# Diff attention: the rows for the maxima taken from the rounded parts of q and k, on 32-row tiles of TensorE

## The chip, the cores and the metric

The kernel runs on one core of one Trainium2 chip. The metric is the device time of one execution in microseconds (us); less is better. A core has TensorE (matrix products, written to PSUM banks), VectorE, ScalarE, GpSimd and SyncE, each with an instruction queue of its own that it works off in order, and they meet at semaphores.

## What is computed

The reference is a two-layer decoder on x of 4 x 512 x 512 floats: windowed attention, context attention, a table-lookup feed-forward, diff attention, a state-space scan and a mix. The change lies in diff attention alone, which is this (batch 4, T = 512, E = 512, 16 heads; q1, k1, q2, k2 have 16 features per head, v has 32):

```python
qkv = layernorm(x) @ W_attn
lam = exp(dot(lambda_q1, lambda_k1)) - exp(dot(lambda_q2, lambda_k2)) + LAMBDA_INIT
attn1 = einsum('bthd,bshd->bhts', q1, k1) * scale
attn2 = einsum('bthd,bshd->bhts', q2, k2) * scale
score = softmax(attn1 - lam * attn2, axis=-1)
out = einsum('bhts,bshd->bthd', score, v)
return ((1 - LAMBDA_INIT) * out.reshape(B, T, E)) @ W_proj
```

With q1 scaled and q2 scaled by -lam, the difference of the two products is one product over 32 features per head: [q1, -lam q2] against [k1, k2]. The softmax subtracts a row maximum before the exponential; whatever number is subtracted cancels in the quotient, so it need only be near the maximum.

## The kernel before

The stages run one after another with a barrier between them. Diff attention (`stage_diff_attention`) is the fourth of five. It makes one pass for each of the 4 batch entries; in a pass the 16 heads go in 4 groups of 4 heads (HG = 4, E2 = 32 features each, so that 4 heads fill 128 partitions). Three groups are in work at once: while group g gets its scores and its output, the row maxima of group g + 1 are found and q and k of group g + 2 are projected (`project`, L1602). The last groups of a pass do that for the first groups of the next one; the last pass has nothing after it.

q and k of a group come out of `project` with 4 heads on 128 partitions in one PSUM bank each. ScalarE writes the rounded value to the tile hi (`high`, L1741), VectorE the rest to the tile lo (`low`, L1814), which also frees the bank. SyncE then copies, head by head, three blocks of 32 partitions into qs and ks (`stack`, L1579): hi, lo, hi for q against hi, hi, lo for k. So qs and ks hold each head on 96 partitions, and a product over the 96 has nearly full precision in one pass of TensorE. Partition 96 of qs takes the negated row maximum, against ones in ks.

For each group there are 16 row steps, one for each head and each tile of 128 queries (`rows`, L1620): one matmul 96 x 128 against 96 x 512 into one bank. VectorE takes the maximum over its 512 columns (`maxima`, L1829) and frees the bank. When all 16 are there, TensorE transposes the maxima (`negate`, L1630), VectorE negates them (`negated`, L1836), and GpSimd's DMA puts them on partition 96 of qs (L1910). Only then can the scores of that group be made, transposed, with the maximum already subtracted (`columns`, L1638); ScalarE takes the exponential from two score banks of their own, and `weigh` (L1648) multiplies by v and by ones, four heads side by side on 32 columns each.

All of rows, q, k, the transposed maxima, and once a pass the transposed features, the values and the output products share one ring of four PSUM banks (`Ring`, L67): the steps listed in `steps` (L1531) take banks 0, 1, 2, 3, 0, ... in this order, and a step waits on `ring.free` of its bank until the step four places before it has been read out. TensorE's order within a group is written out in `one_pass` (L1663): for st = 0 and 1 it is columns, rows, project (q for st = 0, k for st = 1), columns, weigh over v, columns, rows, weigh over ones; then, after st = 1, negate, and then four more weighs with columns between them. ROWS_AT says which row steps go in each of the four places: 0 and 1 ahead of q, 2 to 6 after it, 7 to 10 ahead of k, 11 to 15 after it. VectorE's order (L1852) is: finish of the group before (`finish`, L1844: the reciprocal of the sums and the product with them), maxima of the first place, low of q, maxima of the second and third place, low of k, maxima of the fourth, negated. In the first group of a pass it then does the layer norm of the next pass, in the second it copies features; the additions to x (L1876) stand at the end of a pass.

Of the kernel before, what the change touches and what calls it, by code (L numbers as in the profile page):

```python
# [24 lines left out]
ALU = mybir.AluOpType  # L25
# [7 lines left out]
P = 128  # L33
# [1454 lines left out]
def stage_diff_attention(core, sb, psum, dram, x, consts, scratch):  # L1488
# [21 lines left out]
    hi = sb("d_hi", [P, 2, T], F32R)  # L1510
# [15 lines left out]
    ROWS_AT = ((0, 2), (2, 7), (7, 11), (11, 16))  # L1526
# [39 lines left out]
    with nc.Block() as block:  # L1566
        @block.sync
        def _(sp):
# [10 lines left out]
            def stack(ring, in_pass, g):  # L1579

                for n, (rows, parts) in enumerate(((qs, (hi, lo, hi)), (ks, (hi, hi, lo)))):
                    b, turn = ring.at(("qk"[n], g), in_pass)
                    sp.wait_ge(ring.free[b], turn + 1)
                    for block_, part in enumerate(parts):
                        for j in range(HG):
                            sp.dma_start(rows[block_ * E2:(block_ + 1) * E2, g * HG + j, :].bitcast(F32),
                                         part[j * E2:(j + 1) * E2, n, :].bitcast(F32)) \
                                .then_inc(stacked[n], 16)
# [11 lines left out]
        def _(pe):  # L1600
# [19 lines left out]
            def rows(ring, in_pass, g, a, z):  # L1620

                for m in range(a, z):
                    j, tt = m // TT, m % TT
                    b, turn = ring.at(("row", g, m), in_pass)
                    pe.wait_ge(ring.free[b], turn)
                    nc.tensor.matmul(banks[b][:], qs[0:3 * E2, g * HG + j, tt * P:(tt + 1) * P],  # L1626
                                     ks[0:3 * E2, g * HG + j, :], start=True, stop=True) \
                        .then_inc(ring.full[b], 1)
# [34 lines left out]
            def one_pass(i, more):  # L1663
                for g in range(GROUPS):
# [3 lines left out]
                    if rows_on:  # L1668
                        for m in range(2):
# [48 lines left out]
            for tt in range(TT):  # L1718
                values(first, 0, tt)
            for m in range(2):  # L1720
# [8 lines left out]
        def _(act):  # L1729
# [11 lines left out]
            def high(ring, in_pass, n, kind, g):  # L1741
# [6 lines left out]
                nc.scalar.activation(hi[:, m, :], banks[b][:], ACT.Copy if m else ACT.Identity,  # L1748
# [52 lines left out]
        def _(dve):  # L1801
# [12 lines left out]
            def low(ring, in_pass, n, kind, g):  # L1814
# [5 lines left out]
                if m == 0:  # L1820
                    ins = nc.vector.scalar_tensor_tensor(
                        out=lo[:, m, :], in0=banks[b][:], scalar=coef[:], in1=hi[:, m, :].bitcast(F32),
                        op0=ALU.mult, op1=ALU.subtract)
                else:
                    ins = nc.vector.tensor_tensor(lo[:, m, :], banks[b][:], hi[:, m, :].bitcast(F32),
# [3 lines left out]
            def maxima(ring, in_pass, g, a, z):  # L1829
                for m in range(a, z):  # L1830
                    b, turn = ring.at(("row", g, m), in_pass)
                    dve.wait_ge(ring.full[b], turn)
                    nc.vector.tensor_reduce(mx[:, g, m // TT, m % TT:m % TT + 1], banks[b][:], AX_X, ALU.max) \  # L1833
# [372 lines left out]
```

## Time and profile before

| | |
|---|---|
| median of 3 runs | 2582.32 us (2578.64 to 2584.28) |
| the profiled execution | 2584.38 us |
| its span in the profile | 2582.6 us |
| TensorE matmuls busy | 88% of the span |
| VectorE busy | 69% |
| ScalarE, GpSimd busy | 36%, 41% |
| diff attention | from about 1870 to 2462 us |

The profile lists instructions by line of the kernel with their duration and the idle time of their engine before them. The timeline lists them in order of time, neighbours of one kind merged: "2134.61 3.60 PE L1608 ... x8" are eight matmuls of line 1608, the first of which starts at 2134.61 us and the last of which ends 3.60 us later. A product of plain floats takes two matmul records for each matmul of the code; one of the rounded type takes one. PE is TensorE, DVE is VectorE.

### The profile page before, as it was taken

To read this page: it belongs to the slowest core of one execution; us is meant where nothing else is said; L and a number is where in the kernel's file an instruction comes from. 1 tells how busy PE (TensorE), PEld (TensorE's weight loads), DVE (VectorE), ACT (ScalarE), POOL (GpSimd) and SP (SyncE) were. 2 spreads that over 40 slices of the span, in tenths; PEclk is the share of its full clock that TensorE was granted. 3 is DMA by queue.
4 is the path that set the end of the run, shared out by engine and by line. 5 is a ranking of instruction groups with operands and counts; after the bars stand their busy time and mean duration, and the time that the engine had idled before them with its cause. 6 is when DMAs were issued, how large, how long until landed. Compare 5 with 4: busy or idle time off the path is not lost. (4 is left out here: it accounts for less than half of the span.)

```text
span 2582.6 us, 24445 instructions
## 1 busy us (share of the span) xinstructions
PE 2262.6 (88%) x6992; PEld 1049.2 (41%) x6992; DVE 1771.1 (69%) x2979; ACT 920.4 (36%) x1759; POOL 1052.6 (41%) x789
## 2 busy tenths in 40 slices
PE   6998998999899777774798989989869999999858
PEld 3554444455455443332243434334333333434224
DVE  1887687688768877773688897987745455554454
ACT  1443323334333323331554636446203323232311
POOL 2453333355333424443598888988700000000033
PEclk9999999999999988886899999999979999999878
DMA  6000000000000022225321222221142222121021
GB/s 245 18 21 17 17 25 21 17 17 21 21 17 25 22 88 82 82 82 198 116 91 53 86 83 82 91 77 62 49 131 50 50 49 49 40 58 34 16 98 53
DMA packets 88746, 158.34 MB, mean 61 GB/s; under 512 B 14912, under 2 KB 42432, under 8 KB 86352
## 3 DMA queue, kind: packets, MB, share of 16 engines
q1 hardware_dynamic: 72256, 139.76, 17.1%
q10 hardware_dynamic: 15888, 17.43, 2.1%
q8 instruction: 34, 0.56, 0.1%
q14 instruction: 56, 0.46, 0.1%
q0 software_dynamic: 512, 0.13, 0.0%
HBM read 101.18 MB, written 30.80 MB: 51 GB/s over the span
## 5 line engine op out<-in xcount | busy, mean ns | idle before, releaser
L1389 PE MATMUL c_bank<-c_xn_t,c_weights 128*128 128x512 f32 (+1 forms) x704 | 326.4, 609 | 21.1 <-ACT c_h_t L1429 19.5
L706 POOL TENSOR_SCALAR a_prob<-a_prob,a_rsum 128x256 f32<-128x256 f32 x256 | 147.1, 594 | 466.8 <-DVE a_rsum L634 466.6
L1287 DVE TENSOR_TENSOR_SCAN s_state<-s_decay,s_state 128x512 f32<-128x512 f32 x256 | 305.0, 1210 | 36.1 <-ACT s_decay L1221 36.1
L1237 POOL TENSOR_TENSOR s_state<-s_b_rows,s_delta_u 128x1024 f32<-128x1024 f32 x128 | 301.2, 2363 | 11.2 <-DMA s_b_rows<-scan_bc 8.8
L1221 ACT ACTIVATE s_decay<-s_delta,s_a 128x512 f32<-128x512 f32 x256 | 173.2, 688 | 296.5 <-DVE s_state L1287 269.4
L438 PE MATMUL a_bank<-a_xn_t,a_wq 128*128 128x512 f32 x512 | 227.2, 592 | 0.0
L521 PE MATMUL a_bank<-a_wo,a_out_t 128*128 128x512 f32 x512 | 222.3, 592 | 0.0
L1910 POOL DMA_DIRECT2D d_qs<-d_neg_t x16 | 8.2, 514 | 515.3 <-DVE d_neg_t L1841 515.3
L549 ACT ACTIVATE a_prob<-a_score,a_neg_m 128x256 f32<-128x256 f32 x256 | 117.8, 476 | 278.8 <-DVE a_neg_m L629 278.6
L320 DVE TENSOR_SCALAR f_picks<-f_mask,f_lut_xor,f_lut 128x260 int32<-128x260 int32 x512 | 202.5, 468 | 9.6 <-DVE f_mask L314 1.1
L1762 ACT ACTIVATE d_prob_t<-d_score 128x512 f32<-128x512 f32 x256 | 139.0, 595 | 194.5 <-PE d_score L1645 193.2
L1389 PEld LDWEIGHTS c_bank<-c_xn_t,c_weights 128*128 128x128 f32 (+1 forms) x704 | 128.7, 190 | 179.6 <-issue 176.8
L330 DVE COPY_PREDICATED f_picks<-f_mask,f_picks 128x260 int32<-128x260 int32 x448 | 177.7, 455 | 25.6
L1833 DVE TENSOR_REDUCE d_mx<-d_bank 128x1 f32<-128x512 f32 x256 | 158.6, 683 | 33.4 <-PE d_bank L1626 31.9
L1399 PE MATMUL c_bank<-c_weights,c_h_t 128*128 128x512 f32 (+1 forms) x352 | 168.7, 624 | 0.0
L1250 POOL TENSOR_TENSOR s_group<-s_group,s_state 128x1024 f32<-128x1024 f32 x64 | 151.8, 2372 | 12.5 <-DVE s_state L1295 12.2
L1295 DVE TENSOR_TENSOR s_state<-s_state,s_c 128x1024 f32<-128x1024 f32 x128 | 152.8, 1194 | 0.0
L521 PEld LDWEIGHTS a_bank<-a_wo,a_out_t 128*128 128x128 f32 x512 | 97.3, 190 | 122.5 <-issue 122.5
L438 PEld LDWEIGHTS a_bank<-a_xn_t,a_wq 128*128 128x128 f32 x512 | 97.3, 190 | 109.6 <-issue 108.1
L458 PE MATMUL a_score<-a_k_t,a_q_t 128*128 128x256 f32 (+1 forms) x512 | 132.2, 362 | 0.0
L1608 PE MATMUL d_bank<-d_xn_t,d_w 128*128 128x512 f32 x256 | 120.1, 615 | 4.0 <-ACT d_xn_t L1734 2.7
L1250 POOL TENSOR_TENSOR s_group<-s_state 128x1024 f32<-128x1024 f32 x32 | 75.2, 2350 | 111.0 <-DVE s_state L1295 110.9
(194 smaller groups left out, 3726.6 us busy)
## 6 DMA issues: line engine op xcount, KB each, us to landing
s_b_rows<-scan_bc SPq DMA_DIRECT2D x64, 512.0 KB, 3.6
f_idx<-in_idx SPq DMA_DIRECT2D x64, 130.0 KB, 2.1
ffn_weights<-f_picks SPq DMA_DIRECT2D x64, 130.0 KB, 1.8
r_factor<-in_factors SPq DMA_DIRECT2D x8, 1024.0 KB, 9.0
d_qs<-d_hi SPq DMA_DIRECT2D x128, 64.0 KB, 2.0
d_ks<-d_hi SPq DMA_DIRECT2D x128, 64.0 KB, 2.0
a_wo<-in_wo_t ACTq DMA_DIRECT2D x1, 4096.0 KB, 15.7
scan_y<-m_d_u SPq DMA_DIRECT2D x4, 1024.0 KB, 3.9
```

What stands on the lines that cost most here:

```text
L320: last = dve.tensor_scalar(picks[:, j, :], mask[:, 0, :], self.lut_xor[:, j:j + 1], self.lut[:, 2 * j:2 * j + 1], ALU.bitwise_and, ALU.bit ...
L330: last = self.nc.vector.copy_predicated(self.picks[:, j, :], self.mask[:, level + 1, :], self.picks[:, j + half, :])
L438: mm = nc.tensor.matmul(banks[b][:], w[:, k, :], xn_t[:, k, :], start=(k == 0), stop=(k == KD - 1))
L521: mm = nc.tensor.matmul(banks[b][:], out_t[:, tt, r * P:(r + 1) * P], wo[:, g * REPS + r, :], start=(r == 0), stop=(r == REPS - 1))
L1221: self.nc.scalar.activation(self.decay[u % 2][:], self.delta[:, h % 2, e, :], ACT.Exp, scale=self.a[:, h % 2 * 2 + e, n:n + 1]).then_inc(s ...
L1237: pool.tensor_tensor(self.state[:, s], row.broadcast_to([P, 2, T]), self.delta_u[:, h % 2], ALU.mult) \
L1250: pool.tensor_tensor(group, old if n == 1 else group, self.state[:, c % self.SLOTS], ALU.add) \
L1287: dve.tensor_tensor_scan(self.state[:, s, e, :], self.decay[u % 2][:], self.state[:, s, e, :], 0.0, ALU.mult, ALU.add).then_inc(self.scann ...
L1295: dve.tensor_tensor(self.state[:, s], self.state[:, s], row.broadcast_to([P, 2, T]), ALU.mult) \
L1389: mm = nc.tensor.matmul(banks[b][0:width[o], :], weights[:, lo:lo + width[o]], xn_t[:, k, :], start=(k == 0), stop=(k == KD - 1))
L1399: mm = nc.tensor.matmul(banks[b][:], h_t[0:width[o], o, tt * P:(tt + 1) * P], weights[0:width[o], W_DOWN + o * D:W_DOWN + (o + 1) * D], st ...
L1833: nc.vector.tensor_reduce(mx[:, g, m // TT, m % TT:m % TT + 1], banks[b][:], AX_X, ALU.max) \
```

## The change

The tile hi is kept twice, for even and odd groups, so that hi of group g + 1 still stands while hi of group g + 2 is written. `stack` copies from the copy of its group, `high` and `low` write and read it. The row steps no longer read qs and ks on 96 partitions; they read hi itself, head j on partitions 32 j to 32 j + 31, as matmuls of 32 rows. Their order is turned: m now runs over the four heads of one query tile first (tt, j = divmod(m, 4)), so that four neighbouring steps lie on four different row tiles of the array, and each writes a bank of its own. The maxima are thus those of the product of the rounded parts. ROWS_AT becomes four places of four steps: 0 to 3 ahead of q, 4 to 7 after it, 8 to 11 ahead of k, 12 to 15 after it. Since the rows now read what ScalarE wrote, TensorE waits for hi_done; the wait for the copies (stacked) stays where it is. The number of matmuls, maxima and copies is the same.

```diff
@@ -1507,7 +1507,7 @@
     coef = sb("d_coef", [P, 1], F32)
     norm = Norm(core, sb, "d")
     xn_t = sb("d_xn_t", [P, KD, T], F32)
-    hi = sb("d_hi", [P, 2, T], F32R)
+    hi = sb("d_hi", [P, 2, 2, T], F32R)
     lo = sb("d_lo", [P, 2, T], F32R)
     qs = sb("d_qs", [P, DH, T], F32R)
     ks = sb("d_ks", [P, DH, T], F32R)
@@ -1523,7 +1523,7 @@
     acc = psum("d_acc", [P, T], F32)
     acc_sum = psum("d_acc_sum", [P, T], F32)
     ROWS = HG * TT
-    ROWS_AT = ((0, 2), (2, 7), (7, 11), (11, 16))
+    ROWS_AT = ((0, 4), (4, 8), (8, 12), (12, 16))
     xn_steps = [("xn", k) for k in range(KD)]
     v_steps = [("v", tt) for tt in range(TT)]
     rows_steps = lambda g, a, z: [("row", g, m) for m in range(a, z)]
@@ -1578,7 +1578,8 @@
 
             def stack(ring, in_pass, g):
 
-                for n, (rows, parts) in enumerate(((qs, (hi, lo, hi)), (ks, (hi, hi, lo)))):
+                high = hi[:, g % 2]
+                for n, (rows, parts) in enumerate(((qs, (high, lo, high)), (ks, (high, high, lo)))):
                     b, turn = ring.at(("qk"[n], g), in_pass)
                     sp.wait_ge(ring.free[b], turn + 1)
                     for block_, part in enumerate(parts):
@@ -1620,12 +1621,12 @@
             def rows(ring, in_pass, g, a, z):
 
                 for m in range(a, z):
-                    j, tt = m // TT, m % TT
+                    tt, j = divmod(m, HG)
+                    head = slice(j * E2, (j + 1) * E2)
                     b, turn = ring.at(("row", g, m), in_pass)
                     pe.wait_ge(ring.free[b], turn)
-                    nc.tensor.matmul(banks[b][:], qs[0:3 * E2, g * HG + j, tt * P:(tt + 1) * P],
-                                     ks[0:3 * E2, g * HG + j, :], start=True, stop=True) \
-                        .then_inc(ring.full[b], 1)
+                    nc.tensor.matmul(banks[b][:], hi[head, g % 2, 0, tt * P:(tt + 1) * P], hi[head, g % 2, 1, :],
+                                     start=True, stop=True).then_inc(ring.full[b], 1)
 
             def negate(ring, in_pass, g):
 
@@ -1666,6 +1667,7 @@
                     rg, pg = (g + 1) % GROUPS, (g + 2) % GROUPS
                     rows_on, proj_on = more or g + 1 < GROUPS, more or g + 2 < GROUPS
                     if rows_on:
+                        pe.wait_ge(hi_done, (n + 2) * 2)
                         for m in range(2):
                             pe.wait_ge(stacked[m], (n + 2) * COPIES + 1)
                     for st in range(TT):
@@ -1717,6 +1719,7 @@
                 pe.wait_ge(w_in[n], 16)
             for tt in range(TT):
                 values(first, 0, tt)
+            pe.wait_ge(hi_done, 2)
             for m in range(2):
                 pe.wait_ge(stacked[m], COPIES + 1)
             rows(first, 0, 0, 0, ROWS)
@@ -1745,7 +1748,7 @@
                 act.wait_ge(stacked[m], n * COPIES + 1)
                 b, turn = ring.at((kind, g), in_pass)
                 act.wait_ge(ring.full[b], turn)
-                nc.scalar.activation(hi[:, m, :], banks[b][:], ACT.Copy if m else ACT.Identity,
+                nc.scalar.activation(hi[:, g % 2, m, :], banks[b][:], ACT.Copy if m else ACT.Identity,
                                      scale=1.0 if m else coef[:]).then_inc(hi_done, 1)
 
             def exponentials(n, st, half):
@@ -1819,10 +1822,10 @@
                 b, turn = ring.at((kind, g), in_pass)
                 if m == 0:
                     ins = nc.vector.scalar_tensor_tensor(
-                        out=lo[:, m, :], in0=banks[b][:], scalar=coef[:], in1=hi[:, m, :].bitcast(F32),
+                        out=lo[:, m, :], in0=banks[b][:], scalar=coef[:], in1=hi[:, g % 2, m, :].bitcast(F32),
                         op0=ALU.mult, op1=ALU.subtract)
                 else:
-                    ins = nc.vector.tensor_tensor(lo[:, m, :], banks[b][:], hi[:, m, :].bitcast(F32),
+                    ins = nc.vector.tensor_tensor(lo[:, m, :], banks[b][:], hi[:, g % 2, m, :].bitcast(F32),
                                                   ALU.subtract)
                 ins.then_inc(ring.free[b], 1)
 
@@ -1830,7 +1833,8 @@
                 for m in range(a, z):
                     b, turn = ring.at(("row", g, m), in_pass)
                     dve.wait_ge(ring.full[b], turn)
-                    nc.vector.tensor_reduce(mx[:, g, m // TT, m % TT:m % TT + 1], banks[b][:], AX_X, ALU.max) \
+                    tt, j = divmod(m, HG)
+                    nc.vector.tensor_reduce(mx[:, g, j, tt:tt + 1], banks[b][:], AX_X, ALU.max) \
                         .then_inc(ring.free[b], 1)
 
             def negated(ring, in_pass, n, g):
```

## Rows read from the trace of the kernel before

**Rows 1.** The page: TensorE busy, and the granted clock in 40 slices.

```profile
PE 2262.6 (88%) x6992; PEld 1049.2 (41%) x6992; DVE 1771.1 (69%) x2979; ACT 920.4 (36%) x1759; POOL 1052.6 (41%) x789
...
PEclk9999999999999988886899999999979999999878
```

**Rows 2.** Groups by line, 1870 to 2475 us: busy us, mean ns, idle before, releaser.

```profile
L1833 DVE TENSOR_REDUCE d_mx<-d_bank 128x1 f32<-128x512 f32 x256 | 158.6, 683 | 33.4 <-PE d_bank L1626 31.9
...
L1626 PE MATMUL d_bank<-d_ks,d_qs 96*128 96x512 f32 x256 | 82.3, 421 | 3.5
...
L1635 PE MATMUL d_bank<-ident,d_mx 128*16 128x128 f32 x16 | 4.4, 277 | 16.3 <-DVE d_mx L1833 16.3
```

**Rows 3.** Windows of 30 us: width, busy of PE, PEld, DVE, ACT, POOL, PEclk, DMA.

```profile
2150.00:2180.00 30.00, 27.46 (x127) 10.73 (x125) 18.54 (x26) 10.79 (x20) 0.49 (x1) 1.00 0.26 62
```

**Rows 4.** Timeline of TensorE, third group of the second pass: start, length, what.

```profile
2134.61 3.60 PE L1608 MATMUL d_bank<-d_xn_t,d_w 128*128 128x512 f32 x8
...
2140.31 1.68 PE L1626 MATMUL d_bank<-d_ks,d_qs 96*128 96x512 f32 x5
2141.92 1.06 PE L1659 MATMUL d_acc_sum<-d_prob_t,ones 128*32 128x512 f32 x8
2142.91 0.74 PE L1645 MATMUL d_score<-d_qs,d_ks 97*128 97x512 f32 x2
2143.49 1.09 PE L1626 MATMUL d_bank<-d_ks,d_qs 96*128 96x512 f32 x4
2144.68 3.70 PE L1608 MATMUL d_bank<-d_xn_t,d_w 128*128 128x512 f32 x8
...
2149.87 1.68 PE L1626 MATMUL d_bank<-d_ks,d_qs 96*128 96x512 f32 x5
...
2153.53 0.27 PE L1635 MATMUL d_bank<-ident,d_mx 128*16 128x128 f32 x1 [0.99 <-DVE d_mx L1833]
```

**Rows 5.** Timeline of VectorE in the same group.

```profile
2136.34 1.28 DVE L1833 TENSOR_REDUCE d_mx<-d_bank 128x1 f32<-128x512 f32 x2
...
2140.74 5.67 DVE L1833 TENSOR_REDUCE d_mx<-d_bank 128x1 f32<-128x512 f32 x9 [0.91 <-PE d_bank L1626]
...
2150.30 3.08 DVE L1833 TENSOR_REDUCE d_mx<-d_bank 128x1 f32<-128x512 f32 x5 [0.57 <-PE d_bank L1626]
```

**Rows 6.** Timeline, VectorE: fourth group of that pass, its finish and first maxima.

```profile
2159.04 3.36 DVE L1847 RECIPROCAL d_rsum<-d_acc_sum 128x512 f32<-128x512 f32 x1 [4.83 <-PE d_acc_sum L1659]
...
2163.05 1.28 DVE L1833 TENSOR_REDUCE d_mx<-d_bank 128x1 f32<-128x512 f32 x2
```

**Rows 7.** Timeline, TensorE: the rows and q of the fourth group.

```profile
2160.93 0.63 PE L1626 MATMUL d_bank<-d_ks,d_qs 96*128 96x512 f32 x2
2161.40 3.60 PE L1608 MATMUL d_bank<-d_xn_t,d_w 128*128 128x512 f32 x8
```

**Rows 8.** Timeline: second group of that pass, q on TensorE, first maxima on VectorE.

```profile
2106.00 3.60 PE L1608 MATMUL d_bank<-d_xn_t,d_w 128*128 128x512 f32 x8
...
2108.92 1.28 DVE L1833 TENSOR_REDUCE d_mx<-d_bank 128x1 f32<-128x512 f32 x2
```

**Rows 9.** Timeline: first group of that pass, first maxima and q.

```profile
2079.20 1.28 DVE L1833 TENSOR_REDUCE d_mx<-d_bank 128x1 f32<-128x512 f32 x2
2079.22 3.60 PE L1608 MATMUL d_bank<-d_xn_t,d_w 128*128 128x512 f32 x8
```

**Rows 10.** Timeline, VectorE: third group of the last pass, which projects nothing.

```profile
2409.05 8.85 DVE L1833 TENSOR_REDUCE d_mx<-d_bank 128x1 f32<-128x512 f32 x14 [2.25 <-PE d_bank L1626]
```

**Rows 11.** Timeline, TensorE, scan stage: a 32-row matmul between full ones.

```profile
1301.14 0.50 PE L1174 MATMUL s_c<-s_c_parts,s_c_pick 32*128 32x512 f32 x1
1301.57 1.12 PE L1389 MATMUL c_bank<-c_xn_t,c_weights 128*128 128x512 f32 x2
```

**Rows 12.** Windows, TensorE alone: width, busy, PEclk, DMA share, GB/s.

```profile
2402.00:2405.50 3.50, 2.27 (x7) 1.00 0.02 5
2406.00:2409.00 3.00, 3.00 (x12) 0.50 0.00 0
2426.50:2433.00 6.50, 5.88 (x20) 0.50 0.01 3
360.40:366.00 5.60, 2.83 (x19) 1.00 0.16 48
```

**Rows 13.** Timeline, SyncE: the last copies of k, third group.

```profile
2154.74 2.49 SPq L1586 DMA_DIRECT2D d_ks<-d_lo  x4
```

## What the change will do to the time

> **What bounds the kernel now.** Only diff attention is touched. The page says that TensorE is the busiest engine, near full clock from the middle of this stage on [rows 1]. The stretches of the stage narrow it: in 30 us TensorE has 27.5 us of matmuls, VectorE 18.5, ScalarE 10.8 [rows 3]. So TensorE sets the pace, and VectorE, at under two thirds, looks as if it had room. The grouping by line says where TensorE stops: the row matmuls take 82.3 us of records, with 3.5 us of idle time before them, and the transposed maxima (line 1635) have 16.3 us before them, all of it for VectorE's maxima [rows 2]. The timeline of one group then shows how the two engines are tied: TensorE's steps [rows 4] stand beside VectorE's maxima [rows 5]. What has to be read off is which maximum frees the bank of which matmul, since that is what the change moves.
>
> **What TensorE saves.** Row matmuls of 96 rows follow each other by (1.09 - 0.39)/3 = 0.23 us [rows 4], where 0.39 us is the length of one. Sixteen are 3.7 us a group. Four side by side should take the time of one: four sets, 0.9 us. Against that stand the changes of tiling. The only 32-row matmul in the trace occupies TensorE from 1301.14 to 1301.57, 0.43 us instead of 0.23 [rows 11]: 0.2 us to go in and out. The weigh, four tiles of 32 columns beside each other, takes 0.99 us to the next instruction for two times 0.43 us of stream: 0.13 us [rows 4] (0.43 us from q's eight records: 3.60 us less one record of 0.59, over seven). Two of the four sets stand ahead of a projection (two more changes each), two ahead of a weigh (one more), so I take 0.1 us for going in and up to 0.8 us a group in all. Pure TensorE time: -2.8 + 0.8 = -2.0 us a group, some -29 us for the 15 groups whose rows lie inside the passes. This holds only where TensorE doesn't wait, so every place has to be gone through.
>
> **Place 1, ahead of q.** Before, rows 0 and 1 take two banks and q takes a third. After, rows 0 to 3 take all four, and q takes the bank of row 0: it can't start before VectorE has reduced row 0. But VectorE is then in the finish of the group before, which waits for that group's last weigh and stands ahead of the maxima. In the fourth group of the second pass the reciprocal starts at 2159.04, takes 3.36 us, and the first maximum starts at 2163.05 [rows 6], while q started at 2161.40 [rows 7]. One maximum takes 0.68 us [rows 2], and 0.15 us pass from a maximum to the matmul that waits for it (next paragraph). So q starts at 2163.05 + 0.68 + 0.15 = 2163.88, later by 2.48 us. In the third group: 2136.34 + 0.83 = 2137.17 against 2134.61 [rows 4, 5], 2.56 us. In the second group a layer norm stands ahead of the finish too: 2108.92 + 0.83 = 2109.75 against 2106.00, 3.75 us [rows 8]. In the first group no finish, only the last addition to x: 2079.20 + 0.83 against 2079.22, 0.81 us [rows 9]. TensorE has nothing else to do in that time: behind q in its queue stand columns and weigh, ScalarE waits for those, and hi and lo of q come later too.
>
> **Place 2 and k.** Before, k takes the bank of row 7, the sixth of the nine maxima that start at 2140.74 and follow by (5.67 - 0.68)/8 = 0.62 us: 2140.74 + 5 x 0.62 + 0.68 = 2144.52, and k starts at 2144.68 [rows 4, 5]; that is the 0.15 us. After, k takes the bank of row 8, the fifth maximum behind the start of place 2. In the third group place 2 starts 2.56 + 0.1 us later, so the maxima start at 2143.40, and k at 2143.40 + 4 x 0.62 + 0.68 + 0.15 = 2146.71, which is 2.03 us late: 0.53 us are won back. What the sets save on TensorE is worth nothing here, VectorE's maxima are what ends last. Row 7 needs q's bank; its lo is done before place 2 starts, as before.
>
> **Place 4 and negate.** Before, five maxima from 2150.30, after it four, from 2150.30 + 2.03 + 0.1 = 2152.43. The last ends at 2152.43 + 3 x 0.60 + 0.68 = 2154.91, negate starts at 2155.06 against 2153.53 [rows 4, 5]: 1.53 us late, 0.50 us won back. From there the group runs as before, and the next one starts with this delay.
>
> **Sum of the waits.** Second groups 3.75 - 1.03 = 2.72, third 1.53, fourth 2.48 - 1.03 = 1.45, in three passes: 17.1 us. The last pass has one more group with finish and q and without the norm, 1.45. First groups 0.81 - 1.03 = -0.22, four of them, -0.9. The third group of the last pass projects nothing; there fourteen maxima run without a break up to negate [rows 10], and twelve will: -2 x 0.63 + 0.1 = -1.15. Together +16.5 us. The first sixteen rows of the stage are bound by VectorE before and after, 0. The wait on hi_done costs nothing, the wait on the copies beside it comes later. The second copy of hi adds no instruction. The copies of k end by about 2157.2 + 2 [rows 13] and the next group's wait for them is passed at about 2160; low of k moves by 0.5 us more than negate, still hidden.
>
> **The clock.** The new waits are long. The granted clock has fallen in this stage after short work with gaps: from 2402.00 to 2405.50 TensorE is busy 2.27 us of 3.50, waiting for ScalarE and then for the finish; after it, from 2406.00 to 2409.00, the clock is at 0.50, 1.2 instead of 2.4 GHz [rows 12]. Another stretch at 0.50 lasts from 2426.5 to 2433.0. On the other side 2.8 us of idle time between long dense matmuls left the clock at 1.00 [rows 12]. The new wait resembles the first case: ahead of it stand only two columns, a wait for ScalarE and the set of rows, then 2.5 us or more of nothing. I take it that the clock falls in most of the ten waits of 2.4 us and more. The price by the rows: at half clock for about 3.4 us, 1.7 us of matmuls are lost; for 6.8 us, 3.4. With 1.7 us each, 17 us; bounds 0 and 34.
>
> **The sum.** 16.5 + 17 = 33.5 us. On the profiled execution, 2584.4 us (span 2582.6), that gives 2618; on the median of the runs, 2582.3, 2616.
>
> The Trainium skill has two pages on this. "TensorE: Matmul & The Clock Gate", Part 3, gives 3.07 times the speed for four 32-row tiles of 512 columns; no row tiles stand side by side in this trace, and by it alone the rows' TensorE time would shrink to a third. "TensorEngine Tiling (Array Packing)", under PSUM Bottleneck, says that tiling makes TensorE faster but not the reading of PSUM; the maxima that end last before k and negate agree with it. Its Key Properties say that a change of tiling mode drains TensorE; the 0.2 us around the 32-row matmul agree.
>
> **Rivals.** (1) TensorE alone decides, and the bank of row 0 is free when q wants it: -2.0 us a group, 2582.3 - 29 = 2553 us. For it speaks that TensorE is busy 92% and VectorE 62% [rows 3]. It decides if VectorE's first maximum ends before the set of rows does, about 2161.5 in the fourth group; the finish ends 1.6 us after that point, so this needs another order of VectorE or of the ring than the text of the kernel has. (2) The waits are as above, but the clock doesn't fall: 2582.3 + 16.5 = 2599 us. The last of rows 12 speaks for it. (3) The four tiles don't run beside each other: 4 x 0.23 a set. The weigh behind places 2 and 4 then comes 0.7 us later, inside TensorE's waits for banks and for the last maximum; at most 0.2 us a group get through, 3 us, 2619 us. (4) The clock was hurt elsewhere before and this is better now, and gains and waits cancel: about 2582.
>
> **How the numbers follow.** Forecast with the clock's fall 0.66, rival 2 0.18, rival 1 0.07, rival 3 0.04, rival 4 0.05. The likeliest case runs from 2604 (clock falls in every other wait) to 2633 (the longer price each time). The range takes in rival 2 with 3 us for the settings that I have rounded, and leaves out the top: 2595 to 2628. Faster or slower by over 0.2% is about what a measurement of this kernel can tell from no change. Faster 0.07, within 0.2% 0.05, slower 0.88.
>
> **What would show it.** Right: ahead of q (the weight load or matmul of line 1608) idle time of 2.4 to 3.6 us in ten groups, put down to VectorE's maxima, none over 0.8 in first groups; four row matmuls starting within 0.3 us of each other; idle time ahead of line 1635 up from 16.3 us to some 28 us; stretches at 0.50 of the clock starting at the head of second, third and fourth groups; a distance of about 28 to 30 us between the heads of groups that was 26.8 us. Wrong: q starting right behind the rows, a group under 26.8 us, or the clock at 1.00 throughout. If the sets start 0.1 us apart or more, the tiles load one after another.

## The result and the profile after

The changed kernel takes 2619.57 us, median of 4 runs (2619.26 to 2620.22), against 2582.06 us for the kernel before (4 runs, 2578.64 to 2584.28): the ratio is 1.0147, 95% interval 1.0129 to 1.0164. It is slower by 37.5 us. The forecast was 2616 us in a range of 2595 to 2628. The profiled execution has a span of 2617.5 us against 2582.6.

The page of the changed kernel, its lines for busy time and granted clock, as in [rows 1]:

```profile
PE 2264.1 (86%) x6992; PEld 1027.8 (39%) x6992; DVE 1768.4 (68%) x2979; ACT 919.9 (35%) x1759; POOL 1051.6 (40%) x789
...
PEclk9999999999999988885999999999788999989979
```

All busy times are within about 2% of those before. The work is the same; what grew is the time in which TensorE waits or runs slowly. The page hardly shows the clock's part: in the last third of the span five slices are under 9 where [rows 1] has four.

Groups by line of the changed kernel, 1870 to 2505 us, as in [rows 2] (its lines 1609, 1628, 1636, 1646, 1660 and 1837 are 1608, 1626, 1635, 1645, 1659 and 1833 of the kernel before):

```profile
L1837 DVE TENSOR_REDUCE d_mx<-d_bank 128x1 f32<-128x512 f32 x256 | 157.0, 680 | 35.4 <-PE d_bank L1628 35.1
L1609 PE MATMUL d_bank<-d_xn_t,d_w 128*128 128x512 f32 x256 | 144.4, 718 | 29.9 <-DVE d_mx L1837 25.7 <-ACT d_xn_t L1737 2.7
L1628 PE MATMUL d_bank<-d_hi 32*128 32x512 f32 x256 | 53.3, 505 | 2.6 <-ACT d_v L1742 0.2
L1636 PE MATMUL d_bank<-ident,d_mx 128*16 128x128 f32 x16 | 4.4, 277 | 25.6 <-DVE d_mx L1837 25.6
```

Three things are to be seen. The row matmuls take 29 us less of records than the 82.3 before. The projections now have 29.9 us of idle time ahead of them, 25.7 of it for VectorE's maxima, and their mean record is 718 ns, which is a mixture of matmuls at full and at half clock. The transposed maxima wait 25.6 us instead of 16.3. So what TensorE saves on the rows comes back as waiting.

Timeline of TensorE in the changed kernel, third group of the second pass, to be read against [rows 4]:

```profile
2152.94 0.99 PE L1646 MATMUL d_score<-d_qs,d_ks 97*128 97x512 f32 x2 [0.71 <-ACT d_prob_t L1765]
2153.86 0.51 PE L1628 MATMUL d_bank<-d_hi 32*128 32x512 f32 x4
2156.70 5.28 PE L1609 MATMUL d_bank<-d_xn_t,d_w 128*128 128x512 f32 x8 [2.33 <-DVE d_mx L1837]
...
2164.16 0.51 PE L1628 MATMUL d_bank<-d_hi 32*128 32x512 f32 x4
2164.59 1.06 PE L1660 MATMUL d_acc_sum<-d_prob_t,ones 128*32 128x512 f32 x8
...
2166.26 1.47 PE L1628 MATMUL d_bank<-d_hi 32*128 32x512 f32 x4
2167.82 3.70 PE L1609 MATMUL d_bank<-d_xn_t,d_w 128*128 128x512 f32 x8
...
2173.11 0.51 PE L1628 MATMUL d_bank<-d_hi 32*128 32x512 f32 x4
2176.28 0.27 PE L1636 MATMUL d_bank<-ident,d_mx 128*16 128x128 f32 x1 [1.66 <-DVE d_mx L1837]
```

And VectorE at the head of that group, against [rows 5]:

```profile
2151.97 3.35 DVE L1851 RECIPROCAL d_rsum<-d_acc_sum 128x512 f32<-128x512 f32 x1
2155.35 0.69 DVE L1853 SCALAR_TENSOR_TENSOR d_out_t<-d_acc,d_rsum 128x512 f32<-128x512 f32 x1
2155.96 2.47 DVE L1837 TENSOR_REDUCE d_mx<-d_bank 128x1 f32<-128x512 f32 x4
...
2164.69 4.87 DVE L1837 TENSOR_REDUCE d_mx<-d_bank 128x1 f32<-128x512 f32 x8 [1.09 <-PE d_bank L1628]
```

The four row matmuls are in their banks at 2153.86 + 0.51 = 2154.37. VectorE is in the reciprocal until 2155.32 and in the product until 2156.04, only then does it reduce row 0 and free its bank, and q starts at 2156.70. The first projection takes 5.28 us in place of 3.60, because the clock has fallen. TensorE's windows of the changed kernel there (width, busy, PEclk, DMA share, GB/s):

```profile
2150.00:2156.00 6.00, 3.66 (x24) 1.00 0.00 0
2156.50:2159.50 3.00, 2.80 (x4) 0.50 0.00 0
2160.50:2164.00 3.50, 3.50 (x16) 1.00 0.00 0
```

The clock is at 2.4 GHz while TensorE is busy 61% of the first window, and at 1.2 in the second, right behind the wait.

### The profile page after: what moved, and what is told of

The parts are those of the page before. It is cut to its first block and busy times, and to the rows that moved or that the text cites. A ratio compares the mean times of both kernels' runs of the same rounds, so it can differ in the third digit from the quotient of the medians.

```text
span 2617.5 us, 24461 instructions
## 1 busy us (share of the span) xinstructions
PE 2264.1 (86%) x6992; PEld 1027.8 (39%) x6992; DVE 1768.4 (68%) x2979; ACT 919.9 (35%) x1759; POOL 1051.6 (40%) x789
## 5 line engine op out<-in xcount | busy, mean ns | idle before, releaser
L330 DVE COPY_PREDICATED f_picks<-f_mask,f_picks 128x260 int32<-128x260 int32 x448 | 177.6, 455 | 25.6
L1837 DVE TENSOR_REDUCE d_mx<-d_bank 128x1 f32<-128x512 f32 x256 | 157.0, 680 | 35.4 <-PE d_bank L1628 35.1
L1609 PE MATMUL d_bank<-d_xn_t,d_w 128*128 128x512 f32 x256 | 144.4, 718 | 29.9 <-DVE d_mx L1837 25.7
```

Of the source, the lines that this page charges most:

```text
L330: last = self.nc.vector.copy_predicated(self.picks[:, j, :], self.mask[:, level + 1, :], self.picks[:, j + half, :])
L1837: nc.vector.tensor_reduce(mx[:, g, j, tt:tt + 1], banks[b][:], AX_X, ALU.max) \
```

## The experiments

Each differs in one thing from the kernel before, the changed kernel or another experiment. They are told in the order of the questions. Each ratio is to the kernel before, run beside it; its median lay between 2576.76 and 2583.36 us on these occasions.

**Places or tiles?** The change has two parts: rows read hi on 32-row tiles, and four places of four steps. Each was put alone on the chip. First the places, with the old 96-row matmuls:

```diff
-    ROWS_AT = ((0, 2), (2, 7), (7, 11), (11, 16))     # kernel before
+    ROWS_AT = ((0, 4), (4, 8), (8, 12), (12, 16))
```

> The kernel before (96-row row matmuls on qs and ks, hi kept once) with one edit: the four places take rows 0-3, 4-7, 8-11, 12-15 as in the changed kernel. Theory (place: q waits for the bank of row 0, which stands behind VectorE's finish, and the clock falls in that wait): the 32-row tiles have nothing to do with the loss, so nearly all of it is here too. Waits as in the prediction without 0.1 us a set for the change of tiling, 13 to 16 us, and the clock's fall 10 to 23 us (the wait is shorter by up to 0.5 us, since four rows take 0.9 us of TensorE instead of 0.45): 2605 to 2620 us. Rival (the 32-row tiles or the second copy of hi cost the time): within 5 us of before, 2582.

Measured: 2613.74 us (2611.47 to 2615.70), ratio 1.0128 (1.0107 to 1.0150). Its third group, TensorE's timeline:

```profile
2150.50 1.08 PE L1626 MATMUL d_bank<-d_ks,d_qs 96*128 96x512 f32 x4
...
2153.43 5.40 PE L1608 MATMUL d_bank<-d_xn_t,d_w 128*128 128x512 f32 x8 [1.84 <-DVE d_mx L1833]
```

The result is as expected. There are no 32-row tiles and no second hi here, and yet q waits for the maximum and runs at half clock. The places alone make 33 of the 37.5 us. Then the tiles, with the old places:

```diff
-    ROWS_AT = ((0, 4), (4, 8), (8, 12), (12, 16))     # kernel after
+    ROWS_AT = ((0, 2), (2, 7), (7, 11), (11, 16))
```

> The changed kernel (32-row tiles, hi kept twice, heads side by side) with one edit: the four places are those of before again, rows 0-1, 2-6, 7-10, 11-15. Theory: q has a bank of its own again, no wait for the finish, no fall of the clock; the maxima on VectorE end last before k and negate as before, and TensorE's saving is lost in these waits: 2580 to 2587 us. Rival (TensorE alone decides, so its 2 us a group should show as soon as q does not wait): 2553 to 2560 us. Rival (the tiles cost): 2610 or more.

Measured: 2611.51 us (2609.34 to 2615.18), ratio 1.0120 (1.0098 to 1.0141). This was a surprise: the tiles alone cost about 31 us as well, with q back where it was. The two costs don't add, 33 and 31 make 37.5. Groups by line of this kernel, 1870 to 2500 us:

```profile
L1628 PE MATMUL d_bank<-d_hi 32*128 32x512 f32 x256 | 59.1, 529 | 23.6 <-DVE d_mx L1837 23.2 <-ACT d_v L1742 0.2
...
L1636 PE MATMUL d_bank<-ident,d_mx 128*16 128x128 f32 x16 | 4.8, 297 | 15.3 <-DVE d_mx L1837 15.3
```

The rows themselves now wait 23.2 us for the maxima (the fifth row of a place needs the bank of its first). TensorE's windows around the transposed maxima of the third group, which start at 2163.03, columns as before:

```profile
2160.50:2163.20 2.70, 1.65 (x11) 1.00 0.43 100
2163.60:2166.80 3.20, 3.20 (x12) 0.50 0.43 106
2167.20:2170.00 2.80, 2.80 (x25) 1.00 0.10 23
```

The clock falls here too, at another place: behind negate. In the kernel before, the same passage stayed at 1.00. Seven of the twelve stretches at half clock in this kernel start within about 0.5 us of negate. From 1920 us to the end of the stage TensorE is at half clock for 27.3 us before, 85.3 in this kernel and 81.9 in the changed one.

**Is about half of the loss the clock?** Matmuls were put into the wait ahead of q. They write a score bank whose content is overwritten afterwards, so they do nothing but keep TensorE at work.

```diff
+                        if st == 0 and g and proj_on:
+                            pe.wait_ge(exp_done[0], n * FILLS + 3)
+                            for k in range(5):
+                                nc.tensor.matmul(score[0][:], w[:, k % KD, 0:P], xn_t[:, k % KD, :],
+                                                 start=True, stop=True)
```

> The changed kernel with one addition: ahead of q, in the groups that wait for the finish (second, third, fourth), TensorE does five more matmuls of plain floats, 128 x 512, into a score bank that is free then and is overwritten right after: 5 x 0.43 = 2.1 us of work inside a wait of 2.3 us. Theory: the wait for the bank stays, but the engine is at work in it and the clock stays at 2.4 GHz; what is won is what the clock cost, 17 to 23 us: 2597 to 2603 us. If the clock has no part in the loss: 2620 us, or more where the added matmuls overrun the wait.

Measured: 2621.91 us (2620.54 to 2625.97), ratio 1.0167 (1.0144 to 1.0189). TensorE's timeline, second group of the second pass, and VectorE's at the same place:

```profile
2119.29 4.56 PE L1683 MATMUL d_score<-d_xn_t,d_w 128*128 128x512 f32 x10
2123.69 3.60 PE L1609 MATMUL d_bank<-d_xn_t,d_w 128*128 128x512 f32 x8
```

```profile
2120.89 2.47 DVE L1842 TENSOR_REDUCE d_mx<-d_bank 128x1 f32<-128x512 f32 x4
```

The expectation failed. Five plain-float matmuls are ten records, longer than the wait: q's bank is free at 2120.89 + 0.68 + 0.15 = 2121.72, and q starts at 2123.69, 2.0 us after. Every q behind a filler takes 3.60 us again, but the filler costs what the clock gives back. So it says little on the total. The next kernel has a filler that fits, `range(4 if g == 1 and more else 2)` in place of `range(5)`.

> The changed kernel with matmuls that fit inside q's wait: one matmul of plain floats counts as two records of 0.43 us, so the five of the run before took 4.3 us, not 2.1, and overran the wait by about 1.9 us in each of ten groups. Now four ahead of q in the second group of the first three passes (3.4 us in a wait of 3.5) and two in the other seven groups (1.7 us in 2.3). Theory: q starts where it does in the changed kernel but runs at 2.4 GHz, 22 us are won on its ten projections: 2598 to 2606 us. If the clock has no part in the loss: 2618 to 2622.

Measured: 2607.82 us (2602.75 to 2611.91), ratio 1.0096 (1.0079 to 1.0113), which is 11.8 us less than the changed kernel, and 2 us above the expected range. Third group, TensorE, and the projections over the stage:

```profile
2145.23 0.50 PE L1628 MATMUL d_bank<-d_hi 32*128 32x512 f32 x4
2145.66 1.98 PE L1683 MATMUL d_score<-d_xn_t,d_w 128*128 128x512 f32 x4
2148.07 3.70 PE L1609 MATMUL d_bank<-d_xn_t,d_w 128*128 128x512 f32 x8 [0.42 <-DVE d_mx L1842]
```

```profile
L1609 PE MATMUL d_bank<-d_xn_t,d_w 128*128 128x512 f32 x256 | 122.4, 625 | 8.1 <-DVE d_mx L1842 3.9 <-ACT d_xn_t L1742 2.7
```

q of this group starts 12.26 us after the transposed maxima ahead of it (2135.81 to 2148.07), exactly as in the changed kernel (2144.44 to 2156.70). The projections' records sum to 22.0 us less than in the changed kernel (144.4), with work added rather than removed: the clock, and not the projections, had made them long. Only 11.8 us reach the total. The clock now falls behind negate in six groups (at 1963.1, 2051.9, 2106.5, 2195.3, 2249.9 and 2311.3 us); in the changed kernel it does so in three of them (1965.4, 2207.7 and 2262.3), so three are new. From 1920 us to the end of the stage TensorE is at half clock for 58.0 us against 81.9, and half of that difference is 12.0 us, close to what the total shows. The kernel with the tiles alone has its falls at the same place; so this is most likely the tiles' own cost, coming up where the other is gone.

**What of the tiles' cost is clock?** The same filler, one matmul, ahead of negate, in the kernel with the tiles alone:

```diff
                         if st == 1 and rows_on:
+                            pe.wait_ge(exp_done[0], n * FILLS + 7)
+                            nc.tensor.matmul(score[0][:], w[:, 0, 0:P], xn_t[:, 0, :], start=True, stop=True)
                             negate(ring, i, rg)
```

> The run with the tiles alone (places of before, 2611 us) with one matmul of plain floats, 0.86 us, into a free score bank ahead of negate, where TensorE waits 1.0 us for the last maximum. Theory: most of that run's loss is the clock, which falls about negate because the sets of rows leave TensorE with less to do there; filled, it stays up: 2594 to 2602 us, and what remains over before is the 0.65 us a group for the sets. If the clock is not it, or falls elsewhere: 2608 us or more.

Measured: 2597.86 us (2591.52 to 2601.55), ratio 1.0053 (1.0036 to 1.0069), 13.7 us less than without it, inside the expected range. Four groups, from the transposed maxima of the third group of a pass to those of the next pass, take 137.9 us in both full turns, where the kernel with the tiles alone took 139.8 and 143.8 us and the kernel before 135.4 both times. So 2.5 us a turn, some 0.65 us a group, are not clock. By the distances in the last section they are the changes into and out of the 32-row mode, less what the sets save of TensorE's time. In the last pass the clock still falls.

**Do the tiles cost because they are fast, or because they are 32 rows?** My first reading was that TensorE saves time on the rows, which becomes idle time, and the idle time brings the clock down. If so, 32-row matmuls that are not side by side should cost nothing. Two kernels tried that. One has the tiles but goes head by head, so that neighbours are on the same tile:

```diff
-                    tt, j = divmod(m, HG)          # kernel with tiles, old places; rows and maxima
+                    j, tt = divmod(m, TT)
```

> The run with the tiles alone (32-row tiles, places of before, 2611 us) with one edit: the row steps go head by head again, so that neighbours lie on the same 32-row tile and do not run side by side. It keeps the changes of tiling mode and takes away the time that TensorE saves. Theory (the saved time turns into waits in which the clock falls): the clock stays up, and only the entries into the mode cost, 0.3 to 0.65 us in 15 groups: 2586 to 2592 us, faster than with the rows side by side. If the changes of mode alone cost what the tiles cost: 2605 us or more.

Measured: 2621.82 us (2619.12 to 2622.97), ratio 1.0143 (1.0126 to 1.0160); the expectation failed, and its other branch, 2605 or more, came true. A place still holds rows of two heads, so there remained some overlap, and this kernel did not decide it. The other is the kernel before with one bound changed, from 96 partitions to 32. Its rows read only the rounded parts of the first block (the first 32 of the 96 partitions), so the maxima are those of the changed kernel; all rows are on one and the same tile, none beside another:

```diff
-                    nc.tensor.matmul(banks[b][:], qs[0:3 * E2, g * HG + j, tt * P:(tt + 1) * P],
-                                     ks[0:3 * E2, g * HG + j, :], start=True, stop=True) \
+                    nc.tensor.matmul(banks[b][:], qs[0:E2, g * HG + j, tt * P:(tt + 1) * P],
+                                     ks[0:E2, g * HG + j, :], start=True, stop=True) \
```

> The kernel before with one edit: each row matmul reads only the first 32 of its 96 partitions in qs and ks, that is the rounded parts (partitions 0 to 31 for every head). All of them lie on the same 32-row tile, so none runs beside another and TensorE spends the same 0.22 us on each as before; only the rows used and the tiling mode differ. Theory A (the clock falls because TensorE's time ahead of negate gets shorter): it stays up here, and only the entries into the mode cost, 0.3 to 0.65 us in 15 groups: 2586 to 2594 us. Theory B (a matmul of 32 rows does less for the clock than one of 96 rows that takes the same time; the head-by-head run, 2622 us, points to it): the clock falls about negate here too, 2602 to 2622 us.

Measured: 2616.34 us (2614.75 to 2620.37), ratio 1.0166 (1.0135 to 1.0196). TensorE's timeline, third group of the second pass:

```profile
2165.11 1.77 PE L1626 MATMUL d_bank<-d_ks,d_qs 32*128 32x512 f32 x5
2166.81 1.06 PE L1659 MATMUL d_acc_sum<-d_prob_t,ones 128*32 128x512 f32 x8
...
2168.87 0.37 PE L1635 MATMUL d_bank<-ident,d_mx 128*16 128x128 f32 x1 [0.99 <-DVE d_mx L1833]
```

This is inside the range of Theory B. The wait ahead of line 1635 is 0.99 us, as in [rows 4]. The places themselves are longer: five row matmuls take 1.70 us to the next instruction, against 1.61 in [rows 4], and in place 2 the columns ahead of them 0.80 instead of 0.71. Between transposed maxima (line 1635) without a fall of the clock lie 27.62 and 29.64 us where the kernel before has 26.69 and 28.71: 0.93 us a group for four places, 0.23 us a place, is the price of going into the 32-row mode and out of it. In 15 groups that is some 14 us of the 40 that this kernel loses to the kernel before. The rest is the clock. TensorE's windows at this place, first of the kernel before and then of this one; the first row of each pair is the 3.40 us up to the transposed maxima:

```profile
2150.13:2153.53 3.40, 2.31 (x13) 1.00 0.35 82
2153.50:2160.00 6.50, 6.08 (x39) 1.00 0.34 80
```

```profile
2165.47:2168.87 3.40, 2.32 (x13) 0.93 0.40 94
2168.50:2175.00 6.50, 6.13 (x25) 0.50 0.35 82
```

TensorE's records fill the same time ahead of the transposed maxima (2.32 us of 3.40 against 2.31; over 6.60 us 5.52 against 5.51), and its clock falls all the same, at 2168.4, 0.5 us ahead of them: 25 matmuls in the next window where there were 39. Over the stage it is 88.7 us at half clock against 27.3. So it is shown that 32-row matmuls cost the clock here though none runs beside another, though TensorE saves no time by them, and though there is neither a second hi nor a wait on hi_done: my first reading was wrong, and the second copy of hi is not needed for the loss. Side by side, in the kernel with the tiles alone, they cost less (31 us) than on one tile. Two causes stay open, since no run parts them: the number of rows at work, and the changes of mode, four in and four out in each group, in which TensorE has records but may do less.

**Are there better places?** Three rows ahead of q leave the fourth bank to q, so that q waits for no maximum, and place 4 has one row less ahead of negate. First in the changed kernel:

```diff
-    ROWS_AT = ((0, 4), (4, 8), (8, 12), (12, 16))     # kernel after
+    ROWS_AT = ((0, 3), (3, 8), (8, 12), (12, 16))
```

> The changed kernel with the places at rows 0-2, 3-7, 8-11, 12-15: three rows ahead of q, so that q takes the fourth bank. Theory: no wait for the finish, clock up; k waits for six maxima behind the start of place 2 as before the change, negate for four in place 4 instead of five, so 0.5 us a group are won on before: 2574 to 2580 us. If the loss comes from aligned sets of four or from the tiles: 2600 or more.

Measured: 2593.81 us (2588.57 to 2597.67), ratio 1.0053 (1.0034 to 1.0072). It takes 26 us off the changed kernel by one number, which confirms what the bank of row 0 costs, but it stays above the expectation and above the kernel before; the clock is at half for 41.0 us. The same places with the 96-row matmuls:

> The kernel before (96-row row matmuls) with the places at rows 0-2, 3-7, 8-11, 12-15. It stands to the run with three rows ahead of q on 32-row tiles (2594 us) as before to after, with the tiles alone between them. Theory now (the tiles cost about 0.65 us a group, since the first row of a set is ready 0.1 us later and TensorE's saved time turns into waiting, in which the clock falls): here neither happens, and one maximum less stands ahead of negate: 2572 to 2579 us. If the tiles cost nothing and the places are to blame: 2590 to 2597.

Measured: 2575.24 us (2566.11 to 2578.62, 9 runs), ratio 0.9972 (0.9959 to 0.9984), as expected. What is late then is negate:

```profile
L1635 PE MATMUL d_bank<-ident,d_mx 128*16 128x128 f32 x16 | 4.4, 277 | 16.1 <-DVE d_mx L1833 16.1
```

Nothing needs the transposed maxima until the columns of the next group, so negate was moved back. First behind columns(n, g, 3, 0):

```diff
                             columns(n, g, st + 1, 0)
+                        if st == 2 and rows_on:
+                            negate(ring, i, rg)
...
-                        if st == 1 and rows_on:
-                            negate(ring, i, rg)
```

> The run before the last but one (96 rows, three ahead of q) with negate moved behind the two columns that follow it, so that they fill the wait for the last maximum. Theory: negate's wait, 1.0 us in each of 15 groups less what is left of it behind 0.67 us of columns, goes, and the scores of the next group, which wait for the stored maxima, still find them: 2560 to 2567 us. If another wait takes its place: 2572 to 2579.

Measured: 2566.24 us (2565.30 to 2571.88), ratio 0.9946 (0.9929 to 0.9962), inside the expected range. A wait of 6.1 us is left at negate. Then one step further, behind the weigh over v of st = 2:

```diff
                         weigh(n, g, st, 0)
+                        if st == 2 and rows_on:
+                            negate(ring, i, rg)
...
-                        if st == 1 and rows_on:
-                            negate(ring, i, rg)
```

> 96 rows, three ahead of q, and negate moved once more, behind the weigh over v that follows the two columns, so that TensorE does not wait for the last maximum at all. Theory: what was left of the wait (0.3 us in 15 groups) goes, 2560 to 2565 us, unless the stored maxima now come too late for the scores of the next group: then 2566 or more.

Measured: 2563.64 us (2561.72 to 2566.85), ratio 0.9919 (0.9902 to 0.9935), inside the expected range, the fastest kernel here and faster than the kernel before and the changed one. Groups by line, 1870 to 2475 us:

```profile
L1645 PE MATMUL d_score<-d_qs,d_ks 97*128 97x512 f32 x256 | 104.4, 484 | 14.8 <-DMA d_ks<-d_lo 8.5 <-ACT d_prob_t L1762 3.3 <-DMA d_qs<-d_neg_t 2.9
...
L1635 PE MATMUL d_bank<-ident,d_mx 128*16 128x128 f32 x16 | 4.5, 282 | 1.7 <-DVE d_mx L1833 1.7
```

Of 16.1 us ahead of negate 1.7 are left. The next late thing is the copies of k: columns wait 8.5 us for them, against 1.0 us with negate in its old place. The same two moves on the 32-row tiles:

> The same two moves on the changed kernel's 32-row tiles side by side. With 96 rows a group took 26.4 us, 1.0 us of it waiting at negate; with tiles 26.9 us, 1.65 us of it waiting. Theory: with that wait gone both come to 25.3 us, TensorE's saving now just pays for the changes of mode and k still waits for its bank; and there is no long wait left for the clock to fall in: 2560 to 2570 us. If TensorE's saving shows in full once nothing waits at negate: 2545 to 2555. If the clock still falls in the waits ahead of k: 2575 or more.

Measured: 2570.17 us (2566.37 to 2581.71, 9 runs), ratio 0.9957 (0.9941 to 0.9972), 0.2 us above the upper edge of the expectation. Beside each other, medians in us, by the number of rows in the four places:

| places, negate | 96 rows | 32-row tiles |
|---|---|---|
| 2, 5, 4, 5 | 2582.1 | 2611.5 |
| 4, 4, 4, 4 | 2613.7 | 2619.6 |
| 3, 5, 4, 4 | 2575.2 | 2593.8 |
| 3, 5, 4, 4, negate late | 2563.6 | 2570.2 |

In no order that was tried are the tiles the faster ones.

## Why the prediction was right, point by point

**q's wait for the bank of row 0.** Right in place and size. From the columns at a group's head to q (line 1608 before, 1609 after), third group: 2156.70 - 2152.94 = 3.76 us against 1.29, later by 2.47; forecast 2.56. Second group 3.67 (forecast 3.75), fourth 2.38 (2.48), first 0.89 (0.81). The timeline and the groups by line both put it down to the maxima. The idle time recorded right ahead of q is 2.33 us in the third group, 2.25 in the fourth and 3.53 in the second, close to the forecast's 2.4 to 3.6, and 0.28 in the first, where the forecast said none over 0.8.

**Place 2, k, place 4 and negate.** Forecast: 0.53 us won back at k, 0.50 at negate, 0.10 lost to the tiles at place 2. Measured: from place 2 to k 3.67 us against 4.37, won 0.70; k to place 4 5.29 against 5.19, lost 0.10; place 4 to negate 3.16 (2176.28 - 2173.11) against 3.66, won 0.50; q to place 2 5.89 against 5.70 in the first group, where the clock holds, lost 0.19. The sum without the clock is 2.76, 1.56 and 1.47 us in the second, third and fourth group (forecast 2.72, 1.53, 1.45), and 0.0 in the first (forecast -0.22). The third group of the last pass gained 2.3 us instead of 1.15. Over the stage: (2.76 + 1.56 + 1.47 - 0.02) x 3 + 1.5 - 2.3 = 16.5 us. The forecast was 16.5. Part of that agreement is luck. The first groups and the last pass are two misses that cancel. And the gain in the last pass is not free of the clock: in that very group the kernel before is at half clock from 2405.9 to 2409.3 us, the changed one nowhere, so up to 1.7 of the 2.3 us can be clock.

**The clock.** Right that it falls in the ten waits; the size was too small. The ten projections q behind them take 5.27 to 6.59 us, 58.8 us in all, where the q of a first group, at full clock, takes 3.70 (2094.40 to 2098.10): 21.8 us, where the forecast had 1.7 us each, 17. I had taken a stretch of 3.4 us as the normal case, from the two of [rows 12]; in five of the ten it was 6.8 us. The fault is in the term's size: the rows held both prices, and I took the lower one for all. One sum beside it is wrong: the lower end of the likeliest case, the clock falling in every other wait, is 2582.3 + 16.5 + 8.5 = 2607 us by its own terms and not 2604.

**What took back the rest.** 16.5 + 21.8 = 38.3 us, but the span grew by 34.9. The difference lies behind this stage: the last stage took 118.3 us from the start of the last output product to the end of the span, against 121.8 before. In it TensorE is at half clock for 34.3 us, against 44.4 before; in the last 47 us its granted clock was at 1.00, where it was 0.93 in the last 48 us before. The forecast didn't look there. Within the stage smaller terms of the clock that the forecast left out cancel: 0.5 us more up to the first transposed maxima, 0.8 in the first group and 1.3 where the clock fell at 2207.7, against 2.5 us less behind the last transposed maxima, where the kernel before had been at half clock from 2426.4 to 2433.2. That they cancel is luck too.

**Tiles side by side.** The four matmuls of a set start within 0.01 us of each other (2100.292 to 2100.302, single records), forecast within 0.3. The set takes 0.43 to 0.44 us to the next instruction (2164.16 to 2164.59), four 96-row matmuls 4 x 0.23 = 0.92 [rows 4]: about half. This confirms that the tiles run together, and rules out rival 3. VectorE starts on the first of a set 0.53 us after it began (2164.69 - 2164.16), where it was 0.43 [rows 4, 5]: the first result comes 0.1 us later, as taken. The Trainium skill ("TensorE: Matmul & The Clock Gate", Part 3) gives 3.07 times for such a set; here, to the next instruction, it is 0.92 / 0.43 = 2.1. The Trainium skill's page "TensorEngine Tiling (Array Packing)", PSUM Bottleneck, says that tiling speeds TensorE but not the reading of the banks: the trace agrees, the maxima's records sum to 157.0 us against 158.6, and they are what ends last at q, k and negate.

**Idle time ahead of the transposed maxima.** 25.6 us; forecast some 28, from 16.3.

**Distances.** From negate to negate 29.9 to 33.2 us in the ten groups in which q waits for the finish, 26.7 to 28.7 before; the forecast said 28 to 30 for the distance of the heads, which was low by the clock's longer price.

**The rivals.** (1) TensorE alone decides, 2553 us: excluded by the wait that is in the trace. (2) No fall of the clock, 2599: excluded by the windows, and by the filler, which gave 11.8 us back. (3) Tiles one after another, 2619: its time is nearest to the result, and yet it is wrong, by the starts of the records. A total can't tell it from the forecast. (4) Gains cancel: excluded.

**What the forecast missed though its number held.** It costed the tiles at -2.0 us a group where TensorE sets the pace, and at 0.1 us a place where VectorE does. Alone, they cost 31 us, and with no row matmul beside another 40. In the kernel with the tiles alone the loss divides so: 5.0 us from the first to the fourth transposed maxima, 4.4 over the next four groups, 8.4 over the four after them, 13.1 from there to the last output product. By the kernel with the filler at negate some 10 us of it are changes of mode; the rest goes with the half clock, 85.3 us against 27.3. In the changed kernel that cost is hidden, as its neighbour with the places alone shows: 33 us without the tiles, 37.5 with them. Why so little is added is argued and not shown: where the clock has fallen at q, TensorE is late in any case, and the wait for negate begins in another state. So the number held in part by luck. The mechanism that the forecast names, q's wait for the bank of row 0 and the clock in it, makes 33 of the 37.5 us by itself; that the tiles add only 4 to it the forecast had not claimed.

## What to carry to other kernels

Count banks, not matmuls: in a ring of four, four results ahead of a fifth tie the fifth to the first reader, and if that reader is an engine that has other work ahead in its order, its whole work stands in the path. Saving time on an engine that waits anyway buys nothing, and a wait made longer can lower its clock; look first which wait ends last, and place the producer one bank short of the ring (three rows ahead of q gave 26 us back on the tiles and 38.5 on 96 rows). When a prediction comes true in total, still run its parts alone: here each part cost about 31 to 33 us, and together 37.5.

## What the runs showed of the hardware

- Row matmuls of 32 rows instead of 96, in the same order and at the same lines, cost the kernel 1.66% with nothing side by side. TensorE is at half clock for 88.7 us against 27.3, with records that fill as much of the last 3.4 us ahead of negate (2.32 against 2.31 us). Whether the rows at work or the changes of mode do it is open.
- Matmuls on different row tiles do not start in program order where neighbours share a tile. In the kernel that goes head by head (records told apart by the semaphore of the bank that each one raises), rows 2 and 3 are on the tile of head 0, rows 4 and 5 on that of head 1. Single records start at 2097.407 (row 2), 2097.747 (row 3), 2097.413 (row 4) and 2097.756 (row 5): row 4 starts 0.33 us ahead of row 3, which stands before it in the program. The Trainium skill ("TensorE: Matmul & The Clock Gate", Part 3) says that matmuls start and end in the order of the program; this run differs for the starts.
- Going into the 32-row mode and out of it costs 0.23 us a place, 0.93 us a group of four places, read from the kernel on one tile in groups without a fall of the clock (27.62 against 26.69 us); the 0.2 us that the forecast read off [rows 11] is the same price. In the kernel with the tiles alone some 0.65 us a group are left of it, since the sets save TensorE's time: q to place 2 is 0.19 us longer, place 2 to k 4.63 against 4.37, k to place 4 0.09 longer, place 4 to negate 3.76 against 3.66. The page "TensorEngine Tiling (Array Packing)" of the Trainium skill, Key Properties, says that a change of the tiling mode drains TensorE; the trace agrees, and this is its price here.
- The fall of the clock moves rather than goes: it was at q in the changed kernel (10 of its 15 stretches in this stage from 1920 us on start within 1.6 us of the start of a q), and with q's wait filled it fell behind negate in three groups where it had held.
